# One layer norm moved three pieces up, the low attention weights behind it, and a third PSUM bank for the pieces behind the first attention

## The reference

```
xn = layernorm(x);  x = x + L0_attn(xn) + L0_ffn(xn)
xn = layernorm(x);  x = x + L1_attn(xn) + L1_ffn(xn)

L0_attn: linear attention, 16 heads of 16, with elu(q)+1 and elu(k)+1, then @ o_w.T + o_b
L0_ffn:  W_up, W_gate, W_down each cut to three values;  (silu(x @ up) * (x @ gate)) @ down
L1_attn: softmax attention, 16 heads of 16, rotary positions on q and k, then @ out_w.T + out_b
L1_ffn:  fwht(x*SU_ug), up and gate matmuls with scales, silu(gate)*up, fwht(h*SU_dp), down matmul
```

## Time and profile before

| | us |
|---|---|
| runs (3): lowest, median, highest | 779.87, 781.52, 783.82 |
| profiled execution, its own time | 779.61 |
| its span, first to last instruction | 777.8 |
| PE busy in the span | 712.5 |
| DVE, ACT, POOL busy | 550.7, 435.9, 288.7 |

### The profile page before, as it was taken

The page is one execution under the profiler, slowest core; times in us unless marked ns, Lnnn a source line. Parts: engine busy times, 40 slices in busy tenths (PEclk is TensorE's granted clock), DMA queues, the critical chain, the costliest instruction groups (busy, mean ns, idle before and its releaser), DMA issues.

```text
span 777.8 us, 10975 instructions
## 1 busy us (share of the span) xinstructions
PE 712.5 (92%) x4190; PEld 446.3 (57%) x4190; DVE 550.7 (71%) x896; ACT 435.9 (56%) x579; POOL 288.7 (37%) x273
## 2 busy tenths in 40 slices
PE   3778898969697979999999999999999999999997
PEld 3657787957456868867767676333333433333444
DVE  4897766675557674667888878888888378888416
ACT  2542223345244444243243333999999899999883
POOL 0156865332314566343344343012224213422510
PEclk9898999998799989999999999999999999999999
DMA  6145101000301345334311002344344345342221
GB/s 247 55 155 186 52 0 55 1 1 1 108 0 40 125 155 196 103 106 146 110 55 55 24 32 72 108 131 132 113 138 140 90 133 172 126 131 84 95 85 55
DMA packets 25704, 74.14 MB, mean 95 GB/s; under 512 B 4604, under 2 KB 5980, under 8 KB 24692
## 3 DMA queue, kind: packets, MB, share of 16 engines
q1 hardware_dynamic: 21124, 65.37, 25.1%
q0 software_dynamic: 3808, 7.60, 3.3%
q10 hardware_dynamic: 720, 0.48, 0.2%
HBM read 54.54 MB, written 23.06 MB: 100 GB/s over the span
## 4 chain that ended last, share of the span: by engine, by line
PE 73%; DVE 13%; ACT 5%; issue 4%; POOL 3%; DMA 1%; SPq 0%; DVEq 0%; ACTq 0%; POOLq 0%
PE PS L734 23%; PE PS L996 16%; PE PS L982 11%; PE PS L740 10%; PE PS L965 6%; PE PS L955 4%; DMA stg<-in_wa 1%; DVE mx L1275 1%; DVE XD L1081 1%; PE PS L814 1%; DVE sg L1213 1%; DVE sg L1204 1%; DVE XL L1088 1%; ACT sg L1415 1%; DVE bst L1066 1%
## 5 line engine op out<-in xcount | busy, mean ns | idle before, releaser
L1461 ACT ACTIVATE P<-PS 128x1024 f32<-128x1024 f32 x256 | 249.0, 1024 | 29.9 <-PE PS L982 29.7
L1282 DVE TENSOR_REDUCE mx<-PS 128x1 f32<-128x512 f32 x300 | 189.1, 682 | 32.1 <-PE PS L965 30.5
L1275 DVE TENSOR_REDUCE mx<-PS 128x2 f32<-128x1024 f32 x106 | 124.8, 1220 | 37.9 <-PE PS L955 37.6
L996 PE MATMUL PS<-P,VV 128*32 128x512 f32 x1024 | 136.5, 605 | 0.1
L1538 POOL TENSOR_TENSOR hl<-sg,hh 128x512 fp32r<-128x512 f32 x64 | 83.1, 1299 | 137.1 <-ACT hh L1423 79.9
L982 PEld LDWEIGHTS PS<-QS,KS 64*128 64x128 f32 x512 | 48.4, 183 | 123.2 <-ACT P L1461 110.2
L982 PE MATMUL PS<-QS,KS 64*128 64x512 f32 x512 | 116.6, 456 | 2.3 <-DVE mx L1275 1.8
L965 PE MATMUL PS<-KM,QM 64*128 64x512 f32 x300 | 81.3, 396 | 0.0
L1417 ACT ACTIVATE sg<-PS,cols 128x512 f32<-128x512 f32 x32 | 22.0, 688 | 83.0 <-PE PS L734 83.0
L734 PE MATMUL PS<-XH,UGH 128*128 128x512 f32 x128 | 54.9, 429 | 5.8 <-ACT us L1426 4.9
L1547 POOL TENSOR_TENSOR sg<-sg,us 128x512 f32<-128x512 f32 x32 | 42.1, 1315 | 37.2 <-ACT us L1426 37.2
(11 more groups left out here) (201 smaller groups left out, 1417.5 us busy)
## 6 DMA issues: line engine op xcount, KB each, us to landing
QM<-scr_q SPq DMA_DIRECT2D x16, 512.0 KB, 4.3
KM<-scr_k SPq DMA_DIRECT2D x16, 512.0 KB, 5.3
QS<-scr_q SPq DMA_DIRECT2D x16, 512.0 KB, 4.3
KS<-scr_k SPq DMA_DIRECT2D x16, 512.0 KB, 5.3
scr_q<-spl SPq DMA_DIRECT2D x24, 256.0 KB, 3.3
scr_k<-spl SPq DMA_DIRECT2D x24, 256.0 KB, 3.6
scr_o<-OE POOLq DMA_DIRECT2D x14, 256.0 KB, 2.7
stg<-in_tern SPq DMA_DIRECT2D x3, 1024.0 KB, 4.8
```

The source lines that it names most:

```text
L996: i = e.matmul(PS[32 * c:32 * c + 32, 7, :], v_head(8 * b + kt, 2 * j + c // 2), P[s % 4][:, chunk(c // 2 + 2 * (c % 2))], start=(kt == 0) ...
L1275: e.tensor_reduce(mx[p % 2][:, :, qt, half], PS[:, b:b + 2, :], AX.X, ALU.max).then_inc(q["mx"], 2)
L1282: e.tensor_reduce(mx[p % 2][:, h, qt, half:half + 1], bank[b], AX.X, ALU.max).then_inc(q["mx"], 1)
L1461: e.activation(P[s % 4][:, half * 1024:(half + 1) * 1024], PS[:, b:b + 2, :].rearrange("p b n -> p (b n)"), ACT.Exp).then_inc(q["ex"], 1)
```

## The change

Seven edits, none of which adds or removes arithmetic:
1. IDN gets a semaphore of its own (`idn`); the first transposes wait for it alone, `signs` for the other three loads.
2. `ln_norm` raises `lnn` after each of its four tiles; PE's `ln_turn` waits tile by tile, and goes tile by tile (both banks of a tile) where it went bank by bank.
3. The two VBB instructions become a piece `spread_vb` of their own, at [0,0,4] where they were at [0,0,21].
4. When the first attention has ended ([0,2,15]) bank 2 joins the ring of `side0`, which goes 0, 1, 2 from there. The pieces behind it change banks: `prep_down(0)` has 2, `ln_turn(5)` 0 and 1, `prep_down(1)` 2, `qk(0,0)` 1 and 2, `ln_turn(6)` 0 and 1, `qk(0,1)` 2 and 0.
5. POOL's part of `prep_attn1` becomes `low_attn1`, put after `prep_down(2)` ([0,2,20]), with `load_gate` behind it.
6. `ln1(1)`, the norm n = 5, begins at step 10 of chunk 2, was 13: `ln_stats(5)` at [0,2,11], `ln_norm(5)` and `bias(1,1)` at [0,2,14], `ln_turn(5)` at [0,2,17]; each was three steps later.
7. POOL's part of `qk` becomes `qk_join`, put later: in `side0` at the second resumption after `qk` (`qk(0,0)` at [0,3,7], join at [0,3,10]; `qk(0,1)` at [0,3,14], join at [0,3,16]; `qk(1,1)` at [1,0,5], join at [1,0,9]), for the last four three steps after `qk`.

```diff
     def qk(c, n, count):
         put("qk", c, n, ps.next(), ps.next())
         yield
-        for _ in range(count):
+        for k in range(count):
             yield
+            if k == 0:
+                put("qk_join", c, n)
         put("qk_split", c, n)
...
                     put("scales")
+                    put("spread_vb")
                     put("load_wa1")
...
+        ps.slots.append(2)
         put("prep_attn1")
-        put("load_gate")
         yield
         for q in range(4):
             put("prep_down", q, ps.next())
             yield
+            if q == 2:
+                put("low_attn1")
+                put("load_gate")
...
-    NORMS = {(0, 2, 2): 0, (0, 2, 13): 1, (0, 3, 8): 2, (1, 0, 5): 3}
+    NORMS = {(0, 2, 2): 0, (0, 2, 10): 1, (0, 3, 8): 2, (1, 0, 5): 3}
...
+        if split and k == split_at - 5:
+            put("qk_join", *split)
         if split and k >= split_at:
...
# tensor, ln_turn
-                e.wait_ge(q["lnn"], n + 1)
                 if n == 0:
-                    e.wait_ge(d["c"], 64)
-                for k, b in enumerate(banks):
-                    for t in range(4):
+                    e.wait_ge(d["idn"], 16)
+                for t in range(4):
+                    e.wait_ge(q["lnn"], 4 * n + t + 1)
+                    for k, b in enumerate(banks):
                         i = e.transpose(bank[b][:, t * 128:(t + 1) * 128], ln_buffer(n)[:, t, k * 128:(k + 1) * 128], IDN[:, :])
-                    i.then_inc(q["lnb"], 1)
-                    freed[b] = q["lnl"], 2 * n + k + 1
+                        if t == 3:
+                            i.then_inc(q["lnb"], 1)
+                            freed[b] = q["lnl"], 2 * n + k + 1
...
# tensor, kv_out
+                freed[2] = q["kvs"], tt // 8 + 1
...
# vector, ln_norm
                 for t in range(4):
-                    o = e.tensor_scalar(ln_buffer(n)[:, t, :], X[:, 4 * c + t, :], mv[i][:, t, 0:1], rstd[i][:, t:t + 1], ALU.subtract, ALU.mult)
-                o.then_inc(q["lnn"], 1)
+                    e.tensor_scalar(ln_buffer(n)[:, t, :], X[:, 4 * c + t, :], mv[i][:, t, 0:1], rstd[i][:, t:t + 1], ALU.subtract, ALU.mult).then_inc(q["lnn"], 1)
...
# vector: spread_vb holds the two VBB instructions of add_vb
# gpsimd: prep_attn1 is renamed low_attn1, qk is renamed qk_join, both as they were
```

More of the change, by code:

```diff
@@ L42 @@
 DMAS = """
-cols c ob wsd x0 x1 x2 x3 st0 st1 cs pad sp0 sp1 sp2 sp3 km0 km1 qm0 qm1 ks0 ks1 qs0 qs1 m0 m1
+cols idn c ob wsd x0 x1 x2 x3 st0 st1 cs pad sp0 sp1 sp2 sp3 km0 km1 qm0 qm1 ks0 ks1 qs0 qs1 m0 m1
 oe0 oe1 num0 num1 rc0 rc1 rs0 rs1 late0 late1 late2 late3 wl y
@@ L1063, in ln_stats @@
                     e.wait_ge(q["lnv"], n - 1)
-                    e.wait_ge(q["lnn"], n - 1)
+                    e.wait_ge(q["lnn"], 4 * (n - 1))
                 for t in range(4):
@@ L1099, in signs @@
                 e.wait_ge(d["cols"], 16)
-                e.wait_ge(d["c"], 64)
+                e.wait_ge(d["c"], 48)
                 a, z = COLS["suu"][0], COLS["sud"][0]
@@ L1123, in tern_cut, with spread_vb, add_vb @@
                 e.scalar_tensor_tensor(t, stg[i][:, js], hi, r32(t), ALU.is_gt, ALU.subtract).then_inc(q["tt"], 1)
-            def add_vb(b):
+            def spread_vb():
                 for k in range(2):
                     e.tensor_scalar(VBB[:, k, :], ONES[:, :], col("vb1", k), None, ALU.mult).then_inc(q["vbb"], 1)
+            def add_vb(b):
                 e.wait_ge(d["ob"], 32)
@@ L1331, in last @@
                         e.tensor_tensor(xs, bank[banks[2 + 2 * cc + i]], xs, ALU.add).then_inc(q["ly"], 1)
-            parts = {f.__name__: f for f in (start, ln_stats, ln_norm, ln_turn, bias, w0l, signs, tern_scale, tern_cut, add_vb, half, scales, kv_in, kv_sums, q0,
+            parts = {f.__name__: f for f in (start, ln_stats, ln_norm, ln_turn, bias, w0l, signs, tern_scale, tern_cut, spread_vb, add_vb, half, scales, kv_in, kv_sums, q0,
                                              kv_sum, att_n, att_t, att_b, gate, up, ffn_end, prep_down, prep_ug, qk, qk_split, max_half, max_join, recip, join, project, last)}
@@ L1343, in start @@
                 e.dma_start(cols[:, :], cols_d).then_inc(d["cols"], 16)
-                for t, src in ((IDN, ident_d), (MASK, mask_d), (HAD, had_d), (BKV, bkv_d)):
+                e.dma_start(IDN[:, :], ident_d).then_inc(d["idn"], 16)
+                for t, src in ((MASK, mask_d), (HAD, had_d), (BKV, bkv_d)):
                     e.dma_start(t[:, :], src).then_inc(d["c"], 16)
@@ L1494, in bias @@
                 xs = X[:, 4 * c:4 * c + 4, :]
-                e.wait_ge(q["lnn"], 4 * layer + c + 1)
+                e.wait_ge(q["lnn"], 4 * (4 * layer + c + 1))
                 if layer == 0:
@@ L1528, in butterfly, with low_attn1 @@
                 e.tensor_tensor(z[:, :, k % 2, :], a[:, :, 0, :], a[:, :, 1, :], ALU.subtract if k % 2 else ALU.add).then_inc(q["bf"], 1)
-            def prep_attn1():
+            def low_attn1():
                 for i, (o, n, H, L) in enumerate(((0, 768, W1H, W1L), (1536, 256, WOH, WOL))):
@@ L1559, in ones_v, with qk_join @@
                     e.memset(VV[:, 4352:4368], 0.0).then_inc(q["vones"], 1)
-            def qk(c, n, *banks):
+            def qk_join(c, n):
                 i = 2 * c + n
@@ L1608, in low @@
                     e.wait_ge(q["fill"], 2)
-            parts = {f.__name__: f for f in (bias, fold, kv_in, q0, butterfly, prep_attn1, up, hidden, ones_v, qk, load_wl, out, recip, times, high, low)}
+            parts = {f.__name__: f for f in (bias, fold, kv_in, q0, butterfly, low_attn1, up, hidden, ones_v, qk_join, load_wl, out, recip, times, high, low)}
             for name, *args in order:
```

## The result

The kernel after the change takes 768.87 us in the median of four runs (768.68 to 769.03); before, on the same chip, 780.73 (a fourth run has joined the three of the table above). The ratio is 0.9845, 95% interval 0.9826 to 0.9865: 12 us faster, and 769 was forecast. The profiled execution's span went from 777.8 to 767.0 us, by 10.8 us; the forecast for a like execution was 12.2.

A forecast was written before the change was run, and what follows sets the result against it. PE's waits before 300 us, and half clock behind them, were taken as all that can move. Terms summed to -12.2 us, from the 781.5 median to 769 (767.4 for a like profiled execution), range 762 to 777.

The forecast's parts named there:

- Start: Chunk 0's first transposes go some microseconds earlier, but ACT copies their result behind W0H: 0, with 0.5 either way.
- VBB: PE's wait of 1.52 us at 107 goes, the wait at 80 grows by 0.47: -1.05 us.
- Tile by tile: At norm 4 the first bank is whole after seven transposes, not four, and `att_b` waits for it: +0.45 us.
- Edits 4 to 6: From `att_b(3,1,1)` to chunk 3's first gate, old waits and half clock go, three shorter waits come: -8.5 us.
- Third bank at qk(0,1): Six matmuls run before the bank 0 wait; PE ends 3.0 us earlier, 2.2 kept when layer 1 begins: -2.2 us.
- The join at [1,0,9]: The 4.16 us wait for `us` at 281.40 goes; VV behind `ones_v` limits what is kept: -2.6 us.
- half clock: New waits come closer together and the clock may fall; one short fall taken: +1.5 us, bounds 0 and 8.1.
- The rest: Later joins leave an `hl` 0.2 earlier at 325 and put one `qk_split` 0.4 behind at 347: +0.2 us.
- (a): Rival: POOL and ACT don't bind behind 281, full 3.0 and 6.3 kept, no clock falls: 763 us, chance 0.16.
- (b): Rival: the clock falls at all three places for as long as before, 8.1 instead of 1.5: 776 us, chance 0.18.
- (d): Rival: the clock, once down near 196, stays down in the prepared weights: 793 us, chance 0.04.
- (c): Rival: norm 5 only moves the wait to the pieces it is put in front of: about 779 us, chance 0.07.

The follow-up runs named there:

- e7: The changed kernel with `ln_turn` back in its old form (waits for all four tiles and all constants, transposes bank by bank): 768.75 us.
- e10: The kernel before with the third bank alone added for the pieces behind the first attention: 776.72 us against 781.33, ratio 0.9938.
- e3: The changed kernel with the low attention weights and `load_gate` back right behind the high ones: 769.55 us.
- e6: The changed kernel with VBB's two instructions back in front of `add_vb`: 772.44 us.
- e9: The changed kernel with layer 0's four joins back behind their products, `ones_v` two pieces later and the v pieces three later: 769.04 us.
- e11: The changed kernel with three of layer 0's four joins back behind their products; those of `qk(1,1)` and layer 1 stay late: 766.82 us.
- e12: The changed kernel with only the joins of `qk(1,1)` and layer 1 late, `ones_v` two pieces later, v pieces three later: 766.04 us.
- e2: The changed kernel without the third bank; norm 5 stays early and the low weights late: 775.03 us.
- e4: The changed kernel with all joins of qk back right behind their products, in both layers: 767.16 us.
- e0: The changed kernel itself, measured and profiled once more: 768.43 us.
- e1: The changed kernel with norm 5 back three pieces later (13 instead of 10); third bank and late low weights stay: 771.52 us.

## Why the prediction was right, and where it was not

- **Start, 0.** Right, by e7 (3.8 us earlier, nothing behind it moved).
- **VBB, -1.05.** Right in its mechanism, -1.4 in size. The wait at 107 went, and that at 80 grew by 0.37 (2.58 to 2.95), not by the 0.47 forecast.
- **Tile by tile, +0.45 at norm 4.** Wrong: it costs 0. `att_b` began 2.42 us after the transposes in before and 2.58 in after, but the 0.16 is the clock, which fell while after's transposes ran (1.38 us). Wherever they took 1.06 to 1.24 us, in the old order (before, e7, e10) and in the new one (e3, e6, e9, e11, e12), it is 2.42; where half clock stretched them to 1.38 to 1.94, it is 2.58 to 3.14. The step that failed is that the first bank binds: ACT's copy of it stands behind `hh` anyway. ACT of before, then PE of e3:

```profile
173.40 0.63 ACT L1423 ACTIVATE hh<-sg 128x512 fp32r<-128x512 f32 x1 [3.35 <-DVE sg L1213]
173.93 1.06 ACT L1359 ACTIVATE XH<-PS 128x512 fp32r<-128x512 f32 x2
```

```profile
171.09 1.15 PE L772 MATMUL PS<-IDN,XD 128*128 128x128 f32 x8 [3.07 <-issue]
173.51 0.58 PE L741 MATMUL PS<-W0H,AH 128*128 128x256 f32 x1 [1.27 <-DVE XL L1096]
```

- **Edits 4 to 6, -8.5.** Measured -8.57, and each wait came as forecast: 0.9, 0.7 and 1.6 against 0.83 (`att_b(3,1,1)` at 184.83, was 185.66, on a clock that is 1.66 earlier), 0.52 and 1.65; XD took 2.37, as in the row of 243.21. The step on `load_gate` held too: 1024 KB landed 5.0 us after issue at 204.5, and `prep_ug(4)` was reached at 214.95. But the reason given for XD, that W1L is gone from beside it, is only half true: the norm's new place alone takes XD away from W1L (e3), and edit 5 was worth nothing here. And without the bank 3.7 of the 8.6 are missing (e2). The bound of 9.8 without the third wait is not what its own terms give: 8.5 + 1.6 = 10.1.
- **Third bank at qk(0,1), -2.2.** The step that failed is its last: that the later join leaves 2.2 of 3.0. The bank alone gives 2.85 (e10) or 2.97 (e2), near the 3.0; but the joins behind cost 2.20 of it (e4), not 0.8, and 0.65 was left. I had followed the join to the products behind it and not looked beside it: it runs while DVE does XD of norm 6, whose 2.36 I carried over unchanged; it took 3.33.
- **The join at [1,0,9], -2.6, and half clock, +1.5.** The wait of 4.16 for `us` went and VV's came, as forecast (2.22 and 0.65; 0.64 and 2.08 in e0), with one fall of the clock. Behind v(2), where it fell in e0, the fall cost 8.05 - 6.46 = 1.6, near the 1.5. Of -1.1 for the two -0.47 was measured, and -0.96 against the run with the joins back. Edit 7 as a whole was forecast to gain and costs: 1.2 us by the marks, 1.3 to 1.7 by the medians.
- **The rest, +0.2.** It lies behind the first score tile, where the clock alone moves more; no run tells it.
- **Where no edit gains.** Between 132 and `att_b` 1.20 us went, all clock: 1.36 because in the profiled execution of before it fell behind the wait at 132 and in that of after it did not (e7 has the fall, e10 has not), less the 0.16 above. Ahead of 74 there are 0.92 more (e0, the same kernel, has 0.05) and behind the first score tile 0.55, with a clock that fell near 475 in after and not in before. These leave after 0.3 too slow, so the edits by the marks give 1.38 + 8.57 + 0.65 + 0.47 = 11.1, and the sum's 12.2 was 1.1 too large. The medians moved by 11.9, with an interval from 10.5 to 13.6 that holds both.
- **Rivals.** (a) fell: ACT and POOL do bind, at VV. (b) and (d) fell: the clock did not come down at 190 to 215, nor from there to 250. The Trainium skill, "TensorE: Matmul & The Clock Gate", section "A second HAM failure mode: psum-queue depth-cycling", says that matmul groups which cycle through PSUM banks with small idle times make the clock fall and rise again; the new waits of 0.52 and 1.65 with a third bank did not do this here, while VV's 2.22 did, with 0.83 granted from 280 to 290. (c) fell, but edits 1 and 2 do nothing, edit 5 nothing beside edit 6, and edit 7 as a whole costs.

## What to carry to other kernels

When a step is moved on one engine, look not only at what is queued behind it but at what the other engine does in the same microseconds: a moved POOL instruction lengthened a DVE norm that nobody had touched. Two edits that remove the same collision do not add up, so price each with the other in place, and split an edit that touches several places before keeping it whole. Before a profile's difference is put down to an edit, compare the stretches whose work is the same in both, and take a second profile of the same kernel: here two of them differed by 0.87 us ahead of 74 and split the same wait for VV the other way round.

## What the runs showed of the hardware

**DVE beside POOL.** The four instructions of XD, always the same work, took 1.38 us with POOL idle (e1), 2.37 beside one `hl`, 3.33 beside `hl` and a join (after), 3.79 beside W1L and what followed it, 4.93 at norm 7 beside `hl`, a join and `sg` (after). What is added to 1.38 is 0.72 to 0.78 of the time for which POOL worked beside it (0.99 of 1.27, 1.95 of 2.71, 2.41 of 3.32, 3.55 of 4.78). The Trainium skill, "SBUF — State Buffer", section "SBUF: two separate sides", says that the port pair which DVE and GpSimd share is an exclusive lock: a GpSimd instruction, or a DVE instruction in a 2-port perf mode or with two SBUF inputs, holds it for its whole length if it starts first, and the other stands still. No row shows in which mode XD runs, so that the lock is the reason is not shown. If POOL held the pair for all of its recorded time, all of that would be added; the rows show three quarters, with spans on POOL that are rough.

**The clock behind the same wait.** Behind the wait of 2.23 us at 132 the granted clock fell in 3 of the 14 profiles (before, e6, e7) and not in 11. The 3 share no edit (e7 has the early VBB, and e10 with the late one kept its clock); it cost 1.4 us. Before, then after, by windows of 1 us (length, PE busy, PEclk, DMA share, GB/s):

```profile
133.00:134.00 1.00, 1.00 (x4) 0.50 0.00 0
134.00:135.00 1.00, 1.00 (x7) 0.50 0.00 0
```

```profile
133.00:134.00 1.00, 1.00 (x7) 1.00 0.00 0
134.00:135.00 1.00, 1.00 (x7) 1.00 0.00 0
```

Near 470 to 488 it was the other way round: it fell in 12 of 14, and not in before and e1, whose last stretches are the shortest (471.81 and 471.32, the others 472.2 and more). And a fall can be free: at 80 to 90 the clock was at 0.83 in the mean in most kernels, but at 1.00 in e6, e9, e11 and e12, which then waited 1.6 us for AL at 92 and had gained nothing by 132; in e7 it also fell at 238 to 242, and `sg` to UGH is 21.44 as in after.
